# Sixteen sequences through six attention layers on one core: projections and feed-forward layers as pairs of 64-row matmuls, all eight PSUM banks as one ring

## The chip, the cores and the metric

One NeuronCore of a Trainium2 chip runs the whole program. The metric is the device time of one execution in microseconds (us), median of several. A measurement of this kernel can tell a change of about 0.3% from none.

## The reference, cut to what matters

Sixteen sequences of 256 tokens with 256 features go through six attention layers with 16 heads of 16 features each. Some layers have a feed-forward part. Cut to one layer:

```python
Q, K, V = x @ Wq.T, c @ Wk.T, c @ Wv.T        # c: the context, or x in self-attention (layers 2 and 4)
scores = einsum("bhqd,bhkd->bhqk", Q, K)      # plus masks: general (0), causal (2), lengths (2, 3)
attn = softmax(scores / sqrt(16))
x = layernorm(x + einsum("bhqk,bhkd->bhqd", attn, V) @ Wo.T)   # no Wo in layers 2 and 3
x = layernorm(x + act(x @ W1.T + b1) @ W2.T + b2)              # layers 1 and 5: 1024 wide, layer 3: 256 wide
```

## The kernel before, in words

A unit is one sequence in one attention layer: `n` runs from 0 to 95, `attention(n)` is `n // 16`. A unit is cut into steps, named by kind, unit and index:

- `xtr`, `xff`, `ctr`, `otr`, `ott`, `pvt`: transposes on TensorE of x, of the layernormed x, of the context, of the attention output (two steps, `otr` 0 and 1), of the scaled output, and of V in layer 0. Four 128x128 matmuls against `ident` each.
- `pq`, `pk`, `pvv`, `opr`: the projections Q, K, V and output.
- `nat` 0 to 7: scores of a pair of heads with queries on the partitions, from which VectorE takes the row maximum (`mx`, line 1307; in layer 0 partly a masked form, line 1301). `st` 0 to 7: the same scores transposed, which ScalarE exponentiates into `pt` (line 1037). Both are matmuls over 64 rows: one head of the pair lies on partitions 0 to 63, the other on 64 to 127, and each head's result goes to a PSUM bank of its own.
- `pvg` 0 and 1: attention times V, in four groups of 32 columns of the array (line 854). `pvout`: ScalarE copies the result to `ote`.
- `e0`: a small product that finds sequence lengths in layers 2 and 3.
- `ff1` 0 to 3, `ff2a` 0 to 2 and `ff2`: the feed-forward layers. In layers 1 and 5 they and in layers 2 and 4 the projections are computed from operands split in a rounded part and a rest, as three matmuls at the rounded precision instead of one in plain float32. In the profile both kinds are called f32. A matmul in plain float32 becomes two MATMUL instructions (two passes), a rounded one becomes one.

So the array is used in three shapes, shown in the profile ahead of the operand sizes: `128*128` (full array: transposes, projections, feed-forward), `64*128` (`nat`, `st`) and `128*32` (`pvg`, `e0`).

The order of the work on every engine is a table, `STEPS`: for each layer each step has a place in units (8 to a unit), and optionally other places for single engines. `plan()` adds `8 * n` and `Order` sorts. A step with a place `"q"` is issued on TensorE in two parts: part 0 at its own place and part 1 at the `"q"` place, so other steps may lie between them. In the kernel before the two parts are the two halves of the output (tokens or features 0 to 127 and 128 to 255), each of 256 columns in the same bank.

PSUM has eight banks of 512 float32 columns. Before, `ps_nat` has two, `ps_st` two, `ps_pv` one, and three are a ring `ps_misc` for all the rest. The next `nat` waits until VectorE has read the last one (`max_done`), the next `st` until ScalarE has read the last one (`exp_done`).

```python
for j in halves:                      # pq, pk in layers 1, 3 and 5, before
    for dk in range(2):
        last = nc.tensor.matmul(bank[:, j * S:(j + 1) * S], wv[:, dk, j * P:(j + 1) * P],
                                src[:, dk, :], start=dk == 0, stop=dk == 1)
```

Of the kernel before, what the change touches and what calls it, by code (L numbers as in the profile page):

```python
# [7 lines left out]
P = 128  # L8
B, S, D, H = 16, 256, 256, 16
HD = D // H  # L10
DF = 4 * D
NA = 6
# [18 lines left out]
MISC = 3  # L31
# [41 lines left out]
def w_pieces(a):  # L73
# [4 lines left out]
    0: [("ldt", 0, -23.0722), ("pq", 0, -10.5145, {"a": -11.9187}), ("pql", 0, -10.1072), ("pk", 0, -8.6981, {"a":  # L78
        -8.6385}), ("pkl", 0, -7.9888), ("kin", 0, -8.2233), ("qin", 1, -5.2344), ("qin", 0, -8.2358), ("kin", 1, -5.7617),
        ("pen", 0, -9.8123), ("pvv", 0, 0.7475, {"d": 0.4579}), ("pvt", 0, 4.2243, {"a": 3.4888}), ("pvt", 1, 7.2243, {"a":  # L80
        4.8512}), ("otr", 0, 17.3689, {"d": 17.0245}), ("pb", 0, 18.5644), ("otr", 1, 17.3875, {"d": 17.0609}), ("ott", 0,
        17.5054), ("opr", 0, 18.8675, {"d": 20.7955}), ("lnA", 0, 21.0455, {"g": 22.5079}), ("lnB", 0, 27.3239, {"g":
        30.4865}), ("nmt", 0, 4.81, {"g": 3.166}), ("pvout", 0, 12.4872), ("pvg", 0, 9.6187, {"q": 9.7016}), ("nmt", 1,
# [8 lines left out]
        ("qin", 1, -7.1117), ("qin", 0, -11.3952), ("kin", 1, -3.887), ("pvv", 0, 0.7691, {"q": 0.7862, "d": 0.6665}),  # L92
# [6 lines left out]
        41.0084, {"g": 45.0372}), ("msk", 0, 48.3061), ("nmt", 0, 4.7887, {"g": 3.2704}), ("pvout", 0, 11.3402), ("pvg", 0,  # L99
# [6 lines left out]
        ("hlo", 0, 28.5643), ("hlo", 1, 28.7505), ("hlo", 2, 31.6121), ("hlo", 3, 32.4921)],  # L106
    2: [("xtr", 0, -15.0784, {"a": -16.1489}), ("xtl", 0, -14.8701), ("pq", 0, -14.096, {"q": -14.0381, "a": -14.8795}),
# [64 lines left out]
def attention(n):  # L172

    return n // B


USERS = {"tld": "s", "wsp": "d", "wld": "s", "ldx": "s", "ldt": "s", "ldn": "s", "pen": "s", "nat": "pd", "st": "pa",
         "nmt": "dg", "pvout": "a", "pvg": "p", "pq": "pad", "pk": "pad", "pql": "d", "pkl": "d", "kin": "s", "qin": "s",
# [42 lines left out]
class Order:  # L221

    def __init__(self, stages):
# [13 lines left out]
        for e, part, *_ in sorted(self.by["p"] + self.by["q"] + freeing, key=lambda s: s[2:]):  # L237
            kind, n, i = e
            if kind in RELEASE:
                del held[RELEASE[kind], n, 0]  # L240
# [1343 lines left out]
```

## Time and profile before

| what | value |
|---|---|
| time, median of 3 runs | 2486.88 us (2486.25 to 2492.78) |
| the profiled execution's own time | 2489.72 us |
| its span, first to last instruction | 2487.9 us |
| mean granted TensorE clock | 0.991 |
| TensorE (PE) busy | 2393.9 us, 96% |
| VectorE (DVE) busy | 1926.6 us, 77% |
| ScalarE (ACT) busy | 1454.0 us, 58% |
| GpSimd (POOL) busy | 1104.9 us, 44% |

A row of the profile names the line of the kernel, the engine, the instruction, output <- inputs, the shape, and how many (x). PE is the matmuls, PEld the weight loads that run beside them. Matmuls overlap in the array: one of 0.28 us can start 0.12 us after the last. So what a group of matmuls costs is read from the end of the group before it (start + duration) to its own end, and is called its step here.

### The profile page before, as it was taken

How to read it: one execution, taken by the hardware profiler on the slowest of the kernel's cores; microseconds unless marked ns; L12 is line 12 of the kernel's file. 1: busy time of each engine (PE TensorE's matmuls, PEld its weight loads, DVE VectorE, ACT ScalarE, POOL GpSimd, SP SyncE). 2: the span in 40 equal slices, each digit the busy share in tenths (PEclk: the TensorE clock that was granted, in tenths of full speed). 3: DMA queues.
4: the chain of work that ended last, by engine and by line, in shares of the span. 5: the costliest groups of instructions: out<-in, count | busy, mean ns of one | idle time of the engine just before them, and what ended most of it. 6: DMA issues, size and time to landing. Idle time of an engine off the chain costs nothing.

```text
span 2487.9 us, 63230 instructions
## 1 busy us (share of the span) xinstructions
PE 2393.9 (96%) x24352; PEld 1855.5 (75%) x24352; DVE 1926.6 (77%) x4308; ACT 1454.0 (58%) x2321; POOL 1104.9 (44%) x1606
## 2 busy tenths in 40 slices
PE   5999999999999989999999999999999999999997
PEld 4766767688888868878776666667777778888886
DVE  6888988877778877777788888878789876666662
ACT  1444444565555544455556677677677777666664
POOL 1333434444444433455445677786445443222220
PEclk8999999999999999999999999999999999999998
DMA  5453343222111111232222322222422221111120
GB/s 168 107 157 89 98 102 81 94 75 67 63 63 63 63 43 48 76 106 87 89 92 94 98 92 83 72 82 91 136 93 99 99 76 63 63 63 63 59 84 13
DMA packets 138379, 208.55 MB, mean 84 GB/s; under 512 B 43857, under 2 KB 52321, under 8 KB 138082
## 3 DMA queue, kind: packets, MB, share of 16 engines
q1 hardware_dynamic: 113506, 201.03, 24.7%
q0 software_dynamic: 24576, 3.49, 1.1%
q8 instruction: 196, 3.21, 0.6%
q14 instruction: 101, 0.83, 0.1%
HBM read 40.70 MB, written 4.19 MB: 18 GB/s over the span
## 4 chain that ended last, share of the span: by engine, by line
PE 68%; DVE 9%; issue 2%; ACT 1%; POOL 1%; DMA 0%; DVEq 0%; ACTq 0%
PE ps_pv L854 9%; PE ps_st L677 8%; PE ps_nat L659 7%; PE ps_misc L770 5%; PE ps_misc L886 3%; DVE mx L1307 3%; PE ps_misc L809 3%; PE ps_misc L919 3%; PE ps_misc L954 2%; PE ps_misc L903 2%; PE ps_misc L865 2%; PE ps_misc L955 2%; PE ps_misc L956 2%; PE ps_misc L921 2%; PE ps_misc L920 2%
## 5 line engine op out<-in xcount | busy, mean ns | idle before, releaser
L1037 ACT ACTIVATE pt<-ps_st 128x1024 f32<-128x1024 f32 (+1 forms) x768 | 760.3, 990 | 656.2 <-PE ps_st L677 367.4
L1428 POOL DMA_DIRECT2D q_st<-shifts_t x768 | 456.4, 599 | 1062.7 <-DVE shifts_t L1319 1062.2
L1307 DVE TENSOR_REDUCE mx<-ps_nat 128x4 f32<-128x1024 f32 x560 | 679.8, 1214 | 185.0 <-PE ps_nat L659 166.6
L659 PE MATMUL ps_nat<-k_st,q_st 64*128 64x256 f32 (+1 forms) x3072 | 353.8, 308 | 36.2 <-DVE mx L1307 20.1
L677 PE MATMUL ps_st<-q_st,k_st 64*128 64x256 f32 (+1 forms) x3072 | 366.5, 317 | 10.0 <-ACT pt L1037 6.2
L854 PE MATMUL ps_pv<-pt,vaug 128*32 128x256 f32 (+1 forms) x6144 | 374.5, 376 | 0.0
L677 PEld LDWEIGHTS ps_st<-q_st,k_st 64*128 64x128 f32 x3072 | 231.5, 185 | 145.2 <-issue 106.3
L659 PEld LDWEIGHTS ps_nat<-k_st,q_st 64*128 64x128 f32 x3072 | 233.4, 186 | 111.3 <-issue 63.9
L854 PEld LDWEIGHTS ps_pv<-pt,vaug 128*32 128x32 f32 x6144 | 171.8, 110 | 124.2 <-ACT pt L1037 7.1
L1086 ACT ACTIVATE hT<-ps_misc,cols 128x256 f32<-128x256 f32 x288 | 121.3, 477 | 130.3 <-PE ps_misc L921 72.4
L919 PE MATMUL ps_misc<-xF_hi,up_hi 128*128 128x256 f32 x512 | 158.1, 309 | 14.1 <-DVE qk L1185 10.9
L1475 POOL TENSOR_TENSOR xn<-xn,tiles 128x512 f32<-128x512 f32 x128 | 165.9, 1296 | 10.0
L1474 POOL TENSOR_TENSOR xn<-xn,tiles 128x512 f32<-128x512 f32 x128 | 168.4, 1316 | 4.0 <-ACT xn L1048 2.6
L954 PE MATMUL ps_misc<-down_hi,hT_r 128*128 128x256 f32 x512 | 157.5, 308 | 7.1 <-DVE hT_r L1224 7.1
L1224 DVE TENSOR_TENSOR hT_r<-hT,hT_r 128x512 fp32r<-128x512 f32 x128 | 91.7, 727 | 72.4 <-ACT hT_r L1086 72.4
L1301 DVE CUSTOM_DVE_ANT_0 ps_nat<-ps_nat,on 128x256 f32<-128x256 f32 x320 | 125.5, 455 | 26.8 <-PE ps_nat L659 26.7
L920 PE MATMUL ps_misc<-xF_hi,weights_lo 128*128 128x256 f32 x512 | 145.8, 285 | 0.0
L921 PE MATMUL ps_misc<-xF_lo,up_hi 128*128 128x256 f32 x512 | 145.6, 284 | 0.0
L955 PE MATMUL ps_misc<-weights_lo,hT_r 128*128 128x256 f32 x512 | 145.2, 284 | 0.0
L956 PE MATMUL ps_misc<-down_hi,hT_r 128*128 128x256 f32 x512 | 144.5, 282 | 0.0
L1043 ACT ACTIVATE ote<-ps_pv 128x512 f32<-128x512 f32 x192 | 114.9, 598 | 41.6 <-PE ps_pv L854 41.6
L1413 POOL TENSOR_SCALAR rstd<-mv 128x2 f32<-128x2 f32 x144 | 32.2, 224 | 224.1 <-DVE mv L1113 219.5
(159 smaller groups left out, 5061.5 us busy)
## 6 DMA issues: line engine op xcount, KB each, us to landing
q_st<-qk SPq DMA_DIRECT2D x576, 128.0 KB
k_st<-qk SPq DMA_DIRECT2D x576, 128.0 KB, 2.1
q_st<-shifts_t POOLq DMA_DIRECT2D x768, 4.0 KB, 1.8
weights<-in_weights SPq DMA_DIRECT2D x19, 512.0 KB, 4.0
cT<-in_ctx_t SPq DMA_DIRECT2D x32, 256.0 KB, 2.8
cn<-in_ctx SPq DMA_DIRECT2D x32, 256.0 KB, 2.7
xT<-in_x_t SPq DMA_DIRECT2D x16, 256.0 KB, 3.2
xn<-in_x SPq DMA_DIRECT2D x16, 256.0 KB, 3.0
```

The source lines that it names most:

```text
L659: return nc.tensor.matmul(ps_nat[:, j, hf, 0:keys], lhs, rhs, start=hf == 0, stop=last)
L677: return nc.tensor.matmul(ps_st[:, j, kh, 0:S - q0], lhs, rhs, start=kh == first, stop=last)
L854: last = nc.tensor.matmul(ps_pv[32 * j:32 * j + 32, c, q0:S], vaug[:, rot, kh, slot, :], pt[:, at_p, side, kh * S:(kh + 1) * S - q0], star ...
L919: nc.tensor.matmul(out, up_hi[dk][:, cut], xF_hi[:, dk, :], start=dk == 0, stop=False)
L920: nc.tensor.matmul(out, lo[:, dk, cut], xF_hi[:, dk, :], start=False, stop=False)
L921: last = nc.tensor.matmul(out, up_hi[dk][:, cut], xF_lo[:, dk, :], start=False, stop=dk == 1)
L954: nc.tensor.matmul(out, h_hi, down_hi[:, ch, :], start=step == 0 and c == 0, stop=False)
L955: nc.tensor.matmul(out, h_hi, lo[:, ch, :], start=False, stop=False)
L956: last = nc.tensor.matmul(out, h_lo, down_hi[:, ch, :], start=False, stop=step == 3 and c == 3)
L1037: nc.scalar.activation(pt[:, g % PT_SLOTS, :, 0:used], ps_st[:].rearrange("p j a b -> p j (a b)")[:, :, 0:used], ACT.Exp, scale=SCALE).the ...
L1307: last = nc.vector.reduce_max(out, ps_nat[:], AX)
L1428: nc.gpsimd.dma_start(rows[:, b], shifts_t[32 * b:32 * b + 32, i, :]).then_inc(split_in[rot][i], 16)
```

## The change

Three things change together.

1. **Pairs of 64 rows.** `WIDE` lists the steps that now use the shape 64*128: beside `nat` and `st` all of `pq`, `pk`, `pvv`, `opr`, `ff1`, `ff2a` and `ff2`. A matmul over 128 rows becomes two over 64 rows, one on partitions 0 to 63, one on 64 to 127. In part 0 (`swap` 0) the upper rows add to output half 0 in the first bank and the lower rows to half 1 in the second bank. In part 1 it is the other way round. Since both row groups write to both banks in turn, part 1 waits on a semaphore (`rows_done`) that the last matmul of part 0 raises; in the long chain `ff2a` 0, 1, 2, `ff2` the steps 1 and 3 wait in this way for steps 0 and 2. Transposes, `pvg` and `e0` keep their shapes.
2. **One ring of eight banks.** `ps` holds all banks. `nat`, `st` and every wide step take two neighbouring banks, the rest one, always those that have been free longest by the order of the table. A step waits for the readers of the steps that last had its banks.
3. **A new table.** All places in `STEPS` change. By the sorting rule of `Order`, the steps of 96 units in the order of TensorE are 3472 (parts counted apart) before and 3536 after, since `pq`, `pk`, `pvv` and `opr` of layer 0 are now in two parts.

On VectorE, the scaling of `otr` in layers 0, 1, 4 and 5 reads the bank in two halves: two reciprocals for one, and outside layer 0 two multiplications for one. Other readers get the same elements from two banks instead of one.

```diff
-MISC = 3
+BANKS = 8
+WIDE = {"nat": range(NA), "st": range(NA), "pq": (0, 1, 2, 3, 4, 5), "pk": (0, 1, 2, 3, 4, 5), "pvv": (0, 1, 2, 3, 4, 5), "opr": (0, 1, 4, 5),
+        "ff1": (1, 3, 5), "ff2": (1, 3, 5), "ff2a": (1, 5)}
...
-        ("nat", 0, 0.1635, {"d": 0.599}), ("st",
-        0, 7.5268, {"a": 7.0873}), ("nat", 1, 1.7018, {"d": 1.7987}), ("st", 1, 8.1236, {"a": 7.4481}), ("nat", 2, 2.5189,
...
+        ("otr", 0, 15.9717, {"d": 16.9916}), ("otr", 1, 17.9472, {"d": 18.3718}), ("ott", 0, 18.7715, {"a": 19.3055}),
+        ("opr", 0, 20.5152, {"q": 20.7535, "d": 20.8617}), ("lnA", 0, 34.6135, {"g": 30.255}), ("lnB", 0, 57.1659, {"g":
...
+                taken = {b for banks in held.values() for b in banks}
+                age = {b: k for k, b in enumerate(turn) if b not in taken}
+                if wide(e):
+                    first = min((b for b in age if b + 1 in age), key=lambda b: (max(age[b], age[b + 1]), b))
+                    banks = [first, first + 1]
+                else:
+                    banks = [min(age, key=age.get)]
+                turn = [b for b in turn if b not in banks] + banks
+                self.before[e] = sorted({last[b] for b in banks if last[b]})
...
-        ps_nat = ctx.enter_context(nc.psum_tensor("ps_nat", [P, 2, 2, S], F32))
-        ps_st = ctx.enter_context(nc.psum_tensor("ps_st", [P, 2, 2, S], F32))
-        ps_pv = ctx.enter_context(nc.psum_tensor("ps_pv", [P, 2, S], F32))
-        ps_misc = ctx.enter_context(nc.psum_tensor("ps_misc", [P, MISC, 512], F32))
+        ps = ctx.enter_context(nc.psum_tensor("ps", [P, BANKS, 512], F32))
...
+                def open_bank(e, part=None):
...
+                    if part == 1 and wide(e):
+                        pe.wait_ge(rows_done, phases[e])
+                    if part != 1:
+                        for old in win.before[e]:
+                            if old[0] == "nat":
+                                pe.wait_ge(max_done, nth(old))
+                            elif old[0] == "st":
+                                pe.wait_ge(exp_done, nth(old))
+                            else:
+                                wait_out(pe, old)
+                    return ps[:, win.bank[e][0], :]
...
+                def both_rows(e, swap, lhs, rhs, start, stop):
+
+                    out = halves_of(e)
+                    if not wide(e):
+                        return nc.tensor.matmul(out[:, swap, :], lhs[swap], rhs[swap], start=start, stop=stop)
+                    for g in range(2):
+                        half, rows = g ^ swap, slice(GROUP * g, GROUP * g + GROUP)
+                        last = nc.tensor.matmul(out[:, half, :], lhs[half][rows], rhs[half][rows], start=start and not swap,
+                                                stop=stop and bool(swap))
+                    return last
...
-                            for j in halves:
-                                for dk in range(2):
-                                    last = nc.tensor.matmul(bank[:, j * S:(j + 1) * S], wv[:, dk, j * P:(j + 1) * P],
-                                                            src[:, dk, :], start=dk == 0, stop=dk == 1)
+                            for dk in range(2):
+                                last = both_rows(e, part, [wv[:, dk, j * P:(j + 1) * P] for j in range(2)], [src[:, dk, :]] * 2,
+                                                 dk == 0, dk == 1)
...
-                            th, quarter = step % 2, step // 2
+                            swap, quarter = (0, 1, 1, 0)[step], step // 2
...
+                            else:
+                                pe.wait_ge(rows_done, phases["ff2a", n, step - 1])
...
-                        link(nc.vector.reciprocal(rec[:, i], bank[:, :, :, HD]))
-                        if a in (2, 3):
+                        if not scaled_out(e):
+                            bank = bank.rearrange("p (f q) g (s w) -> p f q g s w", f=2, w=32)
+                            own = rec[:, i].rearrange("p f (q g s) -> p f q g s", q=2, g=2)
+                            for hf in range(2):
+                                last = nc.vector.reciprocal(own[:, hf], bank[:, hf, :, :, :, HD])
+                            link(last)
+                        else:
...
-                            dst = on[:].rearrange("p f (s d) -> p f s d", d=HD)
-                            last = nc.vector.tensor_tensor(dst[:, :, 8 * i:8 * i + 8, :], src, by, ALU.mult)
```

## Rows read from the trace of the kernel before

**Rows 1.** The page: busy time by engine, and the chain that ended last
```profile
PE 2393.9 (96%) x24352; PEld 1855.5 (75%) x24352; DVE 1926.6 (77%) x4308; ACT 1454.0 (58%) x2321; POOL 1104.9 (44%) x1606
PE 68%; DVE 9%; issue 2%; ACT 1%; POOL 1%; DMA 0%; DVEq 0%; ACTq 0%
```
**Rows 2.** The waits of PE alone: who for, us, times, longest
```profile
PE ps_nat L659 <- DVE mx L1307: 20.1, 28, 2.0
PE ps_misc L919 <- DVE qk L1185: 10.9, 4, 4.1
PE ps_nat L659 <- DMA k_st<-qk: 9.4, 13, 1.7
PE ps_misc L753 <- DMA weights<-in_weights: 8.9, 1, 8.9
PE ps_misc L954 <- DVE hT_r L1224: 7.1, 4, 2.8
PE ps_st L677 <- ACT pt L1037: 6.2, 9, 1.1
```
**Rows 3.** Timeline of PE: start us, duration us, line, matmuls (L954-956 feed-forward, rounded)
```profile
706.01 0.28 PE L955 MATMUL ps_misc<-weights_lo,hT_r 128*128 128x256 f32 x1
706.13 0.28 PE L956 MATMUL ps_misc<-down_hi,hT_r 128*128 128x256 f32 x1
706.34 0.50 PE L659 MATMUL ps_nat<-k_st,q_st 64*128 64x256 f32 x4
706.68 0.39 PE L677 MATMUL ps_st<-q_st,k_st 64*128 64x256 f32 x4
707.00 1.13 PE L770 MATMUL ps_misc<-cT,weights 128*128 128x256 f32 x4
...
709.27 0.28 PE L956 MATMUL ps_misc<-down_hi,hT_r 128*128 128x256 f32 x1
709.38 1.02 PE L770 MATMUL ps_misc<-cT,weights 128*128 128x256 f32 x4
```
**Rows 4.** Timeline of PE at 1403 and at 1412 us: transposes, attention times V
```profile
1402.83 0.59 PE L945 MATMUL ps_misc<-weights,hT 128*128 128x256 f32 x2
1403.26 0.60 PE L831 MATMUL ps_misc<-ident,cn 128*128 128x128 f32 x4
...
1405.00 0.40 PE L659 MATMUL ps_nat<-k_st,q_st 64*128 64x256 f32 x4
1405.33 1.07 PE L854 MATMUL ps_pv<-pt,vaug 128*32 128x256 f32 x16
...
1412.15 0.40 PE L659 MATMUL ps_nat<-k_st,q_st 64*128 64x256 f32 x4
1412.48 0.66 PE L865 MATMUL ps_misc<-ident,ote 128*128 128x128 f32 x4
```
**Rows 5.** Timeline of PE at 714 us and at 881 us: two more shapes
```profile
713.95 0.60 PE L865 MATMUL ps_misc<-ident,ote 128*128 128x128 f32 x4
714.48 1.93 PE L854 MATMUL ps_pv<-pt,vaug 128*32 128x256 f32 x32
...
881.14 0.40 PE L659 MATMUL ps_nat<-k_st,q_st 64*128 64x256 f32 x4
881.47 1.06 PE L780 MATMUL ps_misc<-qk,q0blk 128*32 128x256 f32 x8
```
**Rows 6.** Timeline at 1413 us: VectorE ends, the waiting `nat` starts (in brackets: idle before)
```profile
1413.72 1.22 DVE L1307 TENSOR_REDUCE mx<-ps_nat 128x4 f32<-128x1024 f32 x1
1414.99 0.50 PE L659 MATMUL ps_nat<-k_st,q_st 64*128 64x256 f32 x4 [1.00 <-DVE mx L1307]
```
**Rows 7.** VectorE groups: count, busy us, mean ns, idle before
```profile
L1323 DVE RECIPROCAL rec<-ps_misc 128x16 f32<-128x16 f32 x192 | 47.7, 249 | 49.3 <-PE ps_misc L865 47.7
L1343 DVE TENSOR_TENSOR on<-ps_misc,rec 128x256 f32<-128x256 f32 x96 | 40.8, 425 | 3.4
L1334 DVE TENSOR_TENSOR hbuf<-ps_misc,rec 128x128 f32<-128x128 f32 x64 | 15.6, 286 | 1.1
```
**Rows 8.** Busy us in the layers 0, 3 and 4: length, PE, PEld, DVE, ACT, POOL, clock
```profile
0.00:433.00 433.00, 397.94 (x4162) 284.01 (x4162) 359.51 (x1167) 179.72 (x226) 140.88 (x199) 0.98 0.44 115
...
1290.00:1652.00 362.00, 346.18 (x3146) 243.61 (x3146) 307.86 (x631) 248.29 (x384) 259.72 (x390) 1.00 0.26 87
1652.00:1957.00 305.00, 301.11 (x3036) 228.79 (x3037) 257.37 (x472) 213.15 (x299) 166.51 (x265) 0.99 0.30 101
```

More of the change, by code:

```diff
@@ L174, in attention, with wide @@
     return n // B
+TURNS = ("xtr", "xff", "ctr", "otr", "ott", "pvt")
+def wide(e):
+    return attention(e[1]) in WIDE.get(e[0], ())
 USERS = {"tld": "s", "wsp": "d", "wld": "s", "ldx": "s", "ldt": "s", "ldn": "s", "pen": "s", "nat": "pd", "st": "pa",
@@ L212, in plan @@
     return out
-MISC_KINDS = ("pq", "pk", "pvv", "pvt", "ctr", "e0", "otr", "ott", "opr", "xtr", "xff", "ff1", "ff2a", "ff2")
-RELEASE = {"len": "e0", "pql": "pq", "pkl": "pk", "xtl": "xtr", "xfl": "xff"}
+IN_BANKS = ("nat", "st", "pvg", "pq", "pk", "pvv", "pvt", "ctr", "e0", "otr", "ott", "opr", "xtr", "xff", "ff1", "ff2a", "ff2")
+RELEASE = {"pvout": "pvg", "len": "e0", "pql": "pq", "pkl": "pk", "xtl": "xtr", "xfl": "xff"}
 class Order:
@@ L230, in __init__ @@
         halved = {e for e, *_ in self.by["q"]}
-        self.kinds, self.bank = {}, {}
+        self.kinds, self.bank, self.banks, self.before, self.ready = {}, {}, {}, {}, {}
         for e in self.order:
             self.kinds.setdefault(e[0], []).append(e)
-        uses, held = [0] * MISC, {}
-        turn = list(range(MISC))
-        freeing = [s for s in self.by["d"] if s[0][0] in RELEASE and not (s[0][0] == "xfl" and attention(s[0][1]) == 5)]
+        uses, fills, held, last = [0] * BANKS, [0] * BANKS, {}, [None] * BANKS
+        turn = list(range(BANKS))
+        freeing = [s for s in self.by["a"] + self.by["d"]
+                   if s[0][0] in RELEASE and not (s[0][0] == "xfl" and attention(s[0][1]) == 5)]
         for e, part, *_ in sorted(self.by["p"] + self.by["q"] + freeing, key=lambda s: s[2:]):
@@ L617, in filled, with half_done @@
+                def half_done(e, last):
+                    phases[e] = len(phases) + 1
+                    last.then_inc(rows_done, 1)
                 def filled(e, last, part=None):
-                    if part != 0:
-                        last.then_inc(misc_ready[win.bank[e][0]], 1)
+                    if part == 0 and wide(e):
+                        half_done(e, last)
+                    elif part != 0:
+                        last.then_inc(bank_full[win.bank[e][0]], 1)
                 def need_cT(n):
@@ L806, in _ @@
                         wv = w("v" + str(a), D)
-                        for hf in halves:
-                            for dk in range(2):
-                                last = nc.tensor.matmul(bank[:, hf * D:(hf + 1) * D], src[:, dk, hf * P:(hf + 1) * P],
-                                                        wv[:, dk, :], start=dk == 0, stop=dk == 1)
+                        for dk in range(2):
+                            last = both_rows(e, part, [src[:, dk, hf * P:(hf + 1) * P] for hf in range(2)], [wv[:, dk, :]] * 2,
+                                             dk == 0, dk == 1)
                         filled(e, last, part)
@@ L882, in _ @@
                         wo = w("o" + str(a), D)
-                        for th in halves:
-                            for c in range(2):
-                                lhs = (ot0 if a == 0 else ot)[:, c, th * P:(th + 1) * P]
-                                last = nc.tensor.matmul(bank[:, th * D:(th + 1) * D], lhs, wo[:, c, :], start=c == 0, stop=c == 1)
+                        for c in range(2):
+                            lhs = [(ot0 if a == 0 else ot)[:, c, th * P:(th + 1) * P] for th in range(2)]
+                            last = both_rows(e, part, lhs, [wo[:, c, :]] * 2, c == 0, c == 1)
                         filled(e, last, part)
@@ L924, in _ @@
                         wu = w("u" + str(a), D)
[L925 to L929 removed]
+                        for dk in range(2):
+                            last = both_rows(e, part, [wu[:, dk, (2 * i + c) * P:(2 * i + c + 1) * P] for c in range(2)],
+                                             [xF[:, dk, :]] * 2, dk == 0, dk == 1)
                         filled(e, last, part)
@@ L940, in _ @@
                                 pe.wait_ge(d3_made, 1)
-                            for th in halves:
-                                out = bank[:, th * D:(th + 1) * D]
-                                nc.tensor.matmul(out, ones_b[:], d3_b[:], start=True, stop=False)
-                                for ch in range(2):
-                                    last = nc.tensor.matmul(out, hT[:, ch, th * P:(th + 1) * P], wd[:, ch, :], start=False, stop=ch == 1)
+                            both_rows(e, part, [ones_b[:]] * 2, [d3_b[:]] * 2, True, False)
@@ L957, in _ @@
-                            if kind == "ff2a" and i == 1:
+                                ch = 4 * quarter + c
+                                for at, down in ((4, down_hi), (4, lo), (0, down_hi)):
+                                    for g in range(2):
+                                        th, rows = g ^ swap, slice(GROUP * g, GROUP * g + GROUP)
+                                        last = nc.tensor.matmul(out[:, th, :], hT_r[rows, c + at, th * P:(th + 1) * P], down[rows, ch, :],
+                                                                start=step == 0 and c == 0 and at == 4 and down is down_hi,
+                                                                stop=step == 3 and c == 3 and at == 0)
@@ L958, in _ @@
+                            if step == 1:
                                 last.then_inc(quarter_done, 1)
+                            elif kind == "ff2a":
+                                half_done(e, last)
                         if kind == "ff2":
```

314 lines of the change are left out of this document (163 added, 151 removed), and 113 rows, old and new, of the table STEPS.

## The prediction, made before the changed kernel ran

> **What bounds the kernel now.** I read the page first: PE is busy for 96% of the span and holds 68% of the chain that ended last, no other engine more than 9% [rows 1]. PE's own idle time is 94 us (2487.9 - 2393.9), and its list of waits has nothing large: 20.1 us for the row maxima, 10.9 us for banks that VectorE released late, the rest start-up and small things [rows 2]. So PE's own stream sets the time. What that stream consists of is read from its timeline by steps, end of one group to end of the next.
>
> Rounded matmuls on the full array start 0.12 us apart (706.01, 706.13). `nat` after them ends at 706.84, 0.43 us after 706.41, though it is only two pairs; `st` behind it, in the same shape, ends 0.23 us later. A pair of 64-row matmuls thus takes 0.117 us, the same as one full matmul over the same data, and coming from the full array cost 0.20 us. The Q/K projection in plain float32 behind `st` ends 1.06 us after it, while the same four matmuls behind a full-array step take 0.85 us (710.40 - 709.55): 0.20 us again [rows 3]. Transposes take 0.44 us behind a full-array step and 0.59 us behind `nat`: 0.15 us. `pvg` takes 1.00 us behind `nat` [rows 4], and two of them, 32 matmuls, 1.86 us, so 0.86 us each and 0.14 us for the change [rows 5].
>
> So every change of shape costs PE 0.14 to 0.20 us in which it does nothing useful, and which the page counts as busy, because the last matmuls are still running out. Sorting the old table by the rule of `Order` gives 1647 changes of shape: 770 into 64 rows, 274 into 32 columns, 197 into transposes, 406 into projections and feed-forward on the full array. At the prices above that is some 302 us. All steps at their price within a shape, and these, make about 2354 us; the other 134 us of the span are 13 us before the first matmuls end, 3 us after the last, and 118 us of waits and of the half clock that follows them.
>
> The Trainium skill (TensorEngine Tiling, Key Properties) says that changing the tiling mode drains the engine. The trace agrees and gives the price, 0.14 to 0.20 us.
>
> **The change part by part.**
>
> Fewer changes of shape. The new table, sorted by the same rule, has 1016: 454 into 64 rows, 260 into 32 columns, 302 into transposes, none into full-array projections. That saves 316 x 0.20 + 406 x 0.20 + 14 x 0.14 - 105 x 0.15 = 130.6 us. Every one lies on PE, the engine that sets the end.
>
> The pairs themselves. The 6624 MATMUL instructions of the widened steps become 13248. For rounded operands a pair costs 0.117 us against 0.118, nothing [rows 3]. For plain float32 no 64-row pair is in the trace. Nearest are two plain matmuls in different column groups: `e0`, eight instructions, ends 0.99 us after `nat` (882.53 - 881.54), which is 0.14 us for the change and 0.85 us for four slots of 0.21 us; two at a time, then, at the rate of one [rows 5]. `pvg` runs four at a time at that rate. From below nothing can be gained, since the columns to stream are the same; from above, without overlap, each of 2304 plain instructions would cost 0.215 us more. I take nothing, as the nearest row has it.
>
> The Trainium skill (TensorEngine Tiling, Instruction Overhead) speaks against this: about 60 cycles of overhead for each matmul. By its figure 6624 more would cost 6624 x 60 / 2.4 GHz = 166 us, an estimate. The `nat` and `st` rows show no such cost.
>
> Waiting for itself. Part 1 must not start before part 0 has left the array, and PE gets this from a semaphore of its own. There are 576 such waits (512 second parts, and two in each of 32 `ff2a` chains). No engine of the trace waits for itself in this way on PE, so the price comes from a wait for another: VectorE ends at 1414.94, and the `nat` that waited ends at 1415.49, 0.55 us later, instead of the 0.235 us that its two pairs take in a running stream: 0.315 us [rows 6]. Behind the waiting instruction stands all of PE's queue, since it is in order, with the loads of weights too. From below: at least what a change of shape costs, 0.20 us. I take 0.318 (0.315 for rounded, a little more for plain). Where other steps lie between the parts they cover it. In the new table 319 second parts (or chain steps) follow directly on their first part: `ff1` 115, `pvv` 63, `pq` 52, `pk` 51, `opr` 33, five of the rest. That is 319 x 0.318 = 101.4 us. In 81 more, one `nat` or `st` of 0.235 us lies between and 0.083 us stay open: 6.7 us. The other 176 cost nothing. Sum 108.2 us, and this pays back most of what fewer changes of shape bring. At 0.20 us it would be 64 us.
>
> Together PE gets 22 us shorter. It is not even: by layers 0 to 5 about -2, -5, -18, -7, +3 and +8 us, as layer 5 has many `ff1` and layer 4 short steps.
>
> The ring. `nat` and `st` no longer wait for their one buffer. A wait of 1.00 us as at 1414.99 recurs at one `nat` in each of the 16 units of layer 3 [rows 6], some 16 of the 20.1 us [rows 2]; there the new order gives other banks. But wide steps hold two banks for one, and by the new order the distance from the last user of a bank to the next is in many places about 1.4 us, just above a maximum of 1.22 us [rows 6], as before. Part of what is gained comes back elsewhere. From 118 us of waits I leave 107.
>
> VectorE. Of 192 `otr`, 128 now need a second reciprocal: 128 x 0.249 = 31.9 us. 96 multiplications become two of half the size: 96 x (2 x 0.286 - 0.425) = 14.1 us [rows 7]. So VectorE gets 46 us more, 1973 us or 80% of the new span. The cover is its own idle time; in layers 3 and 4 it is busy for 85% and 84% already (307.86 of 362, 257.37 of 305) [rows 8]. What is late next is `ott` in layer 4, which comes about 1 us after `otr` 1 in the new table, while scaling takes about 1.2 us. I put 6 us on the path for it. The readers on ScalarE get the same number of elements: nothing. GpSimd and the queues for DMA issue the same work at other places, with GpSimd at 44% [rows 1]: nothing.
>
> **The sum**, against the profiled execution: 2489.7 - 130.6 + 108.2 - 11 + 6 = 2462.3 us. The median of the runs shown is 2.8 us below that execution, so 2459.5, say **2460 us**, 1.1% faster.
>
> **The rivals.**
>
> *The order by VectorE (slower).* The same place, VectorE's in-order queue, decides otherwise: it is the second engine, its work grows by 46 us, and PE's idle time next to it was tuned away by placing each `nat` just late enough. If all 46 us and not 6 reach PE, in layers 0, 3, 4 and 5, the time is 2500 us. The change is slower than before from 27 us beyond my term on. For it: 83 to 85% busy in three layers [rows 8]. Against it: PE's three longest waits for VectorE come to 38.1 us now [rows 2], and the self-waits give VectorE time.
>
> *The wait for itself is as cheap as a change of shape.* Then the term is 64 and not 108 us: 2416 us. For it: both let the array run dry. Against it: a semaphore must be raised and seen, and after a change of shape the next load starts before the last matmul has ended.
>
> *The ring takes most waits away.* If of 118 us only 60 stay, with my price for the self-wait: 2460 - 47 = 2413 us. For it: more banks between writer and reader. Against it: most of these waits are at the start, at deliveries by DMA, and at transitions between layers, where a bank is not what is missing [rows 2].
>
> *Pairs don't run side by side in plain float32*, so that the rewriting doesn't do what it says: 2304 x 0.215 = 495 us more, 2955 us; a fixed cost of each added matmul would be in between. If each of the 6624 cost 0.025 us, the time were 2626 us. The Trainium skill's section on instruction overhead, named above, gives about this one. Against both: the rows of `nat`, `st` and `e0` [rows 3, 5].
>
> **How the numbers follow.** My sum 0.50, with a range of its own from 2435 to 2485. VectorE 0.20. Cheap self-wait 0.13. Ring 0.12. Pairs that don't overlap or a cost for each 0.05. The range must take in the cheaper cases, down to 2408, and most of VectorE's, up to 2500; outside are the 0.05 and some of both ends. A measurement of this kernel tells about 0.3%, 7.5 us. Faster by more than that (below 2479): 0.13 and 0.12, most of the 0.50 (0.42), and little of VectorE's (0.03): 0.70. Within: 0.12. Slower: 0.18.
>
> **What would show it.** In the new profile: 30976 MATMUL instructions, the projections all in shape 64*128; a second part directly behind its first ends about 0.32 us later than in a running stream, 400 times; a pair in plain float32 starts 0.215 us after the last. PE shows more idle time than 94 us, as a self-wait may be counted as such. VectorE about 1973 us busy. The prediction is wrong if the self-wait costs 0.20 or 0.4 us, if PE's waits for VectorE grow above 90 us, or if the distance of plain pairs is above 0.22 us.

## The result, and the profile after

The changed kernel takes 2500.03 us (median of 7 runs, 2491.09 to 2502.12), the kernel before, beside it, 2486.88 us (7 runs). The ratio, taken over all runs, is 1.004, 95% interval 1.0023 to 1.0057: 0.4% slower (0.5% by the two medians alone). The forecast was 2460 us, 1.1% faster. The profiled execution took 2500.03 us with a span of 2498.2 us at a clock of 0.992.

The page of the changed kernel: busy time, and the chain that ended last by engine and by line (it answers to [rows 1]).
```profile
PE 2378.1 (95%) x30976; PEld 1894.0 (76%) x30976; DVE 1900.8 (76%) x4532; ACT 1464.1 (59%) x2321; POOL 1104.7 (44%) x1606
PE 83%; DVE 7%; issue 4%; ACT 2%; DMA 2%; SPq 1%; POOL 1%; DVEq 0%; ACTq 0%
```
PE is still what sets the time, more than before (83% of the chain, 68% before). It is busy 16 us less, but its idle time has gone from 94 to 120 us (2498.2 - 2378.1), as the prediction had it. The 30976 matmuls are the number forecast. VectorE has not grown: 1900.8 us, and not 1973.

PE's waits in the changed kernel: who for, us, times, longest (they answer to [rows 2]).
```profile
PE ps L687 <- PE ps L687: 18.7, 118, 0.2
PE ps L687 <- DMA weights<-in_weights: 9.3, 1, 9.3
PE ps L1026 <- DVE hT_r L1299: 5.4, 3, 2.4
PE ps L738 <- DVE mx L1383: 5.2, 6, 2.0
```
PE's largest wait is now for itself. The wait of `nat` for the row maxima has fallen from 20.1 us in 28 places to 5.2 in 6. The 18.7 us are only the part of the self-wait in which no matmul shows; the rest hides in "busy", as the timeline makes plain.

Timeline of PE in the changed kernel at 706 us, `ff1` in rounded numbers, part 1 directly behind part 0:
```profile
705.28 0.50 PE L756 MATMUL ps<-q_st,k_st 64*128 64x256 f32 x4
705.62 0.28 PE L687 MATMUL ps<-xF_hi,up_hi 64*128 64x256 f32 x2
705.73 0.28 PE L687 MATMUL ps<-xF_hi,weights_lo 64*128 64x256 f32 x2
...
706.21 0.28 PE L687 MATMUL ps<-xF_lo,up_hi 64*128 64x256 f32 x2
706.55 0.39 PE L687 MATMUL ps<-xF_hi,up_hi 64*128 64x256 f32 x2
706.77 0.29 PE L687 MATMUL ps<-xF_hi,weights_lo 64*128 64x256 f32 x2
...
709.20 0.50 PE L756 MATMUL ps<-q_st,k_st 64*128 64x256 f32 x4 [0.41 <-ACT hT_r L1161]
709.54 1.03 PE L687 MATMUL ps<-weights,cT 64*128 64x256 f32 x8
```
`ff1` follows `st` without a gap, pairs 0.12 us apart, where the full array had cost 0.20 us at each such place [rows 3]. The plain projection ends 0.87 us after `st` (710.57 - 709.70): four pairs at 0.217 us, side by side as assumed. But between 706.21 and 706.55 lie 0.34 us instead of 0.12, and the pair after is 0.22 us behind. Together that is some 0.33 us lost to the self-wait.

Transposes, `pvg` and `nat` in the changed kernel (they answer to [rows 4, 5]):
```profile
1412.74 0.43 PE L756 MATMUL ps<-q_st,k_st 64*128 64x256 f32 x4
1413.10 0.66 PE L674 MATMUL ps<-ident,cn 128*128 128x128 f32 x4
1413.68 1.93 PE L927 MATMUL ps<-pt,vaug 128*32 128x256 f32 x32
1415.55 0.51 PE L738 MATMUL ps<-k_st,q_st 64*128 64x256 f32 x4
```
Ends at 1413.17, 1413.76, 1415.61 and 1416.06: 0.59 us for the transposes, 1.85 for 32 matmuls of `pvg`, 0.45 for `nat`. These are the prices of before, within 0.02 us.

Groups of VectorE in the changed kernel: count, busy us, mean ns, idle before (they answer to [rows 7]).
```profile
L1419 DVE TENSOR_TENSOR on<-ps,rec 128x128 f32<-128x128 f32 x192 | 46.9, 286 | 3.3
L1403 DVE RECIPROCAL rec<-ps 128x8 f32<-128x8 f32 x256 | 34.9, 178 | 55.8 <-PE ps L674 55.6
L1407 DVE RECIPROCAL rec<-ps 128x16 f32<-128x16 f32 x64 | 15.9, 248 | 2.4 <-PE ps L674 1.4
L1193 DVE TENSOR_SCALAR xn<-xn,mv,rstd 128x256 f32<-128x256 f32 x96 | 35.1, 409 | 0.6
L1329 DVE TENSOR_TENSOR q0col<-qk 128x2 f32<-128x2 f32 x32 | 4.9, 153 | 0.1
```
A reciprocal of half the size costs 178 ns and not 249. By mean durations the split adds 13.6 us there (256 x 0.178 + 64 x 0.248 - 192 x 0.249) and not 31.9, and 14.1 at the multiplications; by busy time, since neighbours overlap, only 3.1 and 6.1 us. The last two rows give back 51 us against the same groups in the kernel before (the last section has why):
```profile
L1118 DVE TENSOR_SCALAR xn<-xn,mv,rstd 128x256 f32<-128x256 f32 x96 | 63.4, 701 | 2.5 <-POOL rstd L1414 1.9
L1254 DVE TENSOR_TENSOR q0col<-qk 128x2 f32<-128x2 f32 x32 | 28.1, 879 | 0.6
```

To see where the time is, every step of PE is priced as in the prediction: end of step minus end of the step before, minus the step's price within its shape, minus the price of a change of shape where there is one. The steps at their own price make 2054.2 us in every kernel of this study. What is left over is sorted by place: at second parts (and second chain steps) directly behind their first; at those with one step between; everywhere else, which is waits for other engines and the half clock behind them (1.2 GHz granted instead of 2.4 for some 45 us before and 39 us after, two thirds of it in the first 47 us, where PE idles until the first transfers land, and in the last 32 us). The 13 to 15 us at both ends are not in it. The table is of the profiled executions; the profiled one of later_fixed_banks is 3.7 us above its median, those of one_wait and no_self_wait are 2.7 and 4.5 us below theirs.

| kernel | median us | changes of shape (us) | directly behind: count, us | one between, us | elsewhere, us |
|---|---|---|---|---|---|
| before | 2486.9 | 1647 (299.8) | none | none | 119.5 |
| the forecast for after | 2460 | 1016 (171.4) | 319, 101.4 | 6.7 | 113 |
| after | 2500.0 | 1016 (171.1) | 319, 138.5 | 14.3 | 106.2 |
| one_wait | 2473.8 | 1016 (171.1) | 319, 110.3 | 7.8 | 112.2 |
| no_self_wait | 2388.4 | 1016 (171.1) | 319, 5.4 | 3.0 | 134.7 |
| one_reciprocal | 2493.3 | 1016 (171.1) | 319, 136.0 | 14.3 | 102.2 |
| both_small | 2471.5 | 1016 (171.1) | 319, 108.6 | 9.0 | 112.8 |
| full_array | 2551.7 | 2097 (388.2) | none | none | 93.7 |
| apart | 2491.0 | 1016 (171.1) | 38, 15.6 | 20.2 | 215.3 |
| later_scores | 2582.8 | 1016 (171.1) | 46, 18.6 | 27.5 | 295.9 |
| later_fixed_banks | 2475.5 | 1016 (171.1) | 46, 17.6 | 32.5 | 188.4 |
| earlier_fixed_banks | 2496.0 | 1016 (171.1) | 85, 30.4 | 16.7 | 207.8 |

The rows of before and after say at once which term is off: the self-wait, 152.8 us and not 108.2. The rest of this text is about why, and about what it would bring to be rid of it.

### The profile page after: what moved, and what is told of

Read it like the earlier page. It is cut to its first block, busy times and chain, and to the rows that moved or that the text cites. A ratio compares the mean times of both kernels' runs of the same rounds, so it can differ in the third digit from the quotient of the medians.

```text
span 2498.2 us, 77552 instructions
## 1 busy us (share of the span) xinstructions
PE 2378.1 (95%) x30976; PEld 1894.0 (76%) x30976; DVE 1900.8 (76%) x4532; ACT 1464.1 (59%) x2321; POOL 1104.7 (44%) x1606
## 4 chain that ended last, share of the span: by engine, by line
PE 83%; DVE 7%; issue 4%; ACT 2%; DMA 2%; SPq 1%; POOL 1%; DVEq 0%; ACTq 0%
PE ps L687 34%; PE ps L927 12%; PE ps L756 9%; PE ps L738 8%; PE ps L674 8%; PE ps L1026 8%; PE ps L746 2%; PE ps L761 2%; DVE mx L1383 1%; DMA q_st<-shifts_t 1%; PE ps L856 1%; DVE qk L1246 1%; DVE stats L1185 1%; ACT hT_r L1161 1%; POOL q_st L1510 0%
## 5 line engine op out<-in xcount | busy, mean ns | idle before, releaser
L1111 ACT ACTIVATE pt<-ps 128x1024 f32<-128x1024 f32 (+1 forms) x768 | 748.5, 989 | 328.0 <-PE ps L746 162.5
L1383 DVE TENSOR_REDUCE mx<-ps 128x4 f32<-128x1024 f32 x560 | 677.3, 1218 | 171.5 <-PE ps L738 167.8
L756 PE MATMUL ps<-q_st,k_st 64*128 64x256 f32 (+1 forms) x3072 | 373.2, 322 | 23.1 <-DMA q_st<-shifts_t 5.3
L927 PE MATMUL ps<-pt,vaug 128*32 128x256 f32 (+1 forms) x6144 | 373.5, 374 | 2.0 <-DVE qk L1258 1.2
L738 PE MATMUL ps<-k_st,q_st 64*128 64x256 f32 (+1 forms) x3072 | 361.2, 313 | 10.3 <-DVE mx L1383 5.2
L756 PEld LDWEIGHTS ps<-q_st,k_st 64*128 64x128 f32 x3072 | 249.1, 186 | 111.9 <-issue 73.8
L738 PEld LDWEIGHTS ps<-k_st,q_st 64*128 64x128 f32 x3072 | 254.2, 187 | 56.2 <-issue 38.9
L927 PEld LDWEIGHTS ps<-pt,vaug 128*32 128x32 f32 x6144 | 177.6, 109 | 123.7 <-issue 15.5
L1026 PE MATMUL ps<-down_hi,hT_r 64*128 64x256 f32 x2048 | 214.6, 288 | 5.7 <-DVE hT_r L1299 5.4
L1026 PEld LDWEIGHTS ps<-down_hi,hT_r 64*128 64x128 f32 x2048 | 175.3, 188 | 10.7 <-DVE hT_r L1299 8.3
```

Of the source, the lines that this page charges most:

```text
L738: return nc.tensor.matmul(scores_of(e)[:, j, hf, 0:keys], lhs, rhs, start=hf == 0, stop=last)
L756: return nc.tensor.matmul(scores_of(e)[:, j, kh, 0:S - q0], lhs, rhs, start=kh == first, stop=last)
L927: last = nc.tensor.matmul(bank[32 * j:32 * j + 32, c * S + q0:(c + 1) * S], vaug[:, rot, kh, slot, :], pt[:, at_p, side, kh * S:(kh + 1) * ...
L1026: last = nc.tensor.matmul(out[:, th, :], hT_r[rows, c + at, th * P:(th + 1) * P], down[rows, ch, :], start=step == 0 and c == 0 and at == ...
L1111: nc.scalar.activation(pt[:, g % PT_SLOTS, :, 0:used], scores_of(e).rearrange("p j a b -> p j (a b)")[:, :, 0:used], ACT.Exp, scale=SCALE) ...
L1383: last = nc.vector.reduce_max(out, found, AX)
```

## Experiments

### What a self-wait costs

**one_wait.** In the changed kernel part 1 of a projection, of `opr`, of `ff1` 0 and of `ff2` in layer 3 waits for `rows_done`, and once more for its source, which part 0 has already waited for. Here part 1 waits for `rows_done` alone.
```diff
-                        if a == 0:
-                            pe.wait_ge(ot0_ready, ...)
+                        if part == 1:
+                            pass
+                        elif a == 0:
+                            pe.wait_ge(ot0_ready, ...)
```


> The changed kernel, but a second part repeats none of the waits that its first part has already passed (for transposes, for the context, for weights); it waits only for rows_done. Theory A (a second wait on the same instruction costs about 0.065 us even when it is long fulfilled): 199 projections and 32 ff1 directly behind their first part start their loads about 0.057 us instead of 0.12 to 0.13 us after its end, some 15 us less than the changed kernel, about 2485 us. Theory B (fulfilled waits are free, the difference between ff1 and the projections comes from plain float32): 2500 us as the changed kernel.

Measured: 2473.84 us, ratio 0.9944 (0.9932 to 0.9957). That is 26 us below the changed kernel and 0.6% faster than before. The theory of a costly second wait holds, that of free fulfilled waits is out; the 15 us expected were too few, since they reckoned with the delay of the load alone. The same second part, `pk` of a unit of layer 4, in three kernels that differ in its waits (the third, further down, also in the bank that each half of the rows adds to). First the changed kernel, matmuls and then weight loads:
```profile
1761.09 0.31 PE L687 MATMUL ps<-xT_hi,weights_lo 64*128 64x256 f32 x2
1761.56 0.39 PE L687 MATMUL ps<-xT_hi,qkv_hi 64*128 64x256 f32 x2
...
1761.53 0.21 PEld L687 LDWEIGHTS ps<-xT_hi,qkv_hi 64*128 64x128 f32 x2 [0.32 <-issue]
```
One_wait:
```profile
1741.11 0.28 PE L687 MATMUL ps<-xT_hi,weights_lo 64*128 64x256 f32 x2
1741.45 0.39 PE L687 MATMUL ps<-xT_hi,qkv_hi 64*128 64x256 f32 x2
...
1741.45 0.19 PEld L687 LDWEIGHTS ps<-xT_hi,qkv_hi 64*128 64x128 f32 x2 [0.27 <-PE ps L687]
```
The last matmul of part 0 ends at 1761.41 and at 1741.39, as the profile models its end. With one wait the next load starts 0.06 us after that end, with two 0.12 us after it, though the second wait was long fulfilled. By all places of this kind, the median of the load's start is 0.056 to 0.070 us after the end with one wait and 0.118 to 0.132 with two. The loss against a running stream is 0.33 to 0.34 us with one wait; with two it is 0.42 us for rounded and 0.50 us for plain operands. In the changed kernel only `ff1` 1 to 3 and the chain steps had one.

**before_self_wait.** The old kernel, on the full array, with the same kind of wait between the two parts of its halved steps and nothing else changed.
```diff
+                    if part == 1:
+                        pe.wait_ge(rows_done, phases[e])
...
-                    if part != 0:
+                    if part == 0:
+                        phases[e] = len(phases) + 1
+                        last.then_inc(rows_done, 1)
+                    else:
```


> The kernel before with one thing added: the second part of pq, pk, pvv, opr, ff1 and ff2 waits on TensorE for the end of its first part; full-array matmuls, old table, old banks. 266 second parts follow directly on their first part. Theory A (the wait for itself costs what the changed kernel shows, 0.33 us where it is the only wait and 0.42 us where another, long fulfilled wait stands beside it): about 98 x 0.33 + 168 x 0.42 = 103 us more, about 2590 us. Theory B (the price is that of a change of shape, 0.20 us, and the rest of the changed kernel's time is in something else): 53 us more, 2540 us. Theory C (the time lies with VectorE, and pauses of TensorE are absorbed by waits that it has anyway): under 30 us more.

Measured: 2567.40 us, ratio 1.0322 (1.0308 to 1.0336), 80.5 us more. At the 266 second parts directly behind their first stand 97.1 us, 0.365 each (0.33 with one wait, 0.39 with two); some 17 us are missing again at other waits. So the price of a single wait, 0.33 us, has nothing to do with pairs or the ring, and the 0.20 us of a change of shape is excluded. With two waits the full array loses less (0.39) than the pairs (0.42 and 0.50).

**no_self_wait.** one_wait without any of the 576 self-waits. So that nothing has to wait, a row group adds to the same bank in both parts; every output half then is a sum over the wrong operands.
```diff
-                        last = nc.tensor.matmul(out[:, half, :], lhs[half][rows], rhs[half][rows], ...
+                        last = nc.tensor.matmul(out[:, g, :], lhs[half][rows], rhs[half][rows], ...
```


> one_wait with all 576 self-waits gone, in its order and with its banks. So that nothing has to wait, each row group adds to the same bank in both parts (the lower rows always to the first bank, the upper rows always to the second), so that every output half gets the sum over the wrong operands; matmuls, shapes, loads and readers are the same in number and size. In one_wait the self-waits cost 118 us by their places (110.3 behind their own first part, 7.8 with one step between). If TensorE's stream alone sets the time, all of it comes back: 2473.8 - 118 = 2356 us. Rival (the other engines are hardly behind TensorE, and what a self-wait gives back is waited for elsewhere, as in later_fixed_banks, where 68 us less at second parts brought 0 us): over 2450 us. In between, the share that comes back is read off: half of it is 2415.

Measured: 2388.37 us, ratio 0.9609 (0.9592 to 0.9627), 85.5 us below one_wait. The same `pk`:
```profile
1685.00 0.31 PE L685 MATMUL ps<-xT_hi,weights_lo 64*128 64x256 f32 x2
1685.11 0.32 PE L685 MATMUL ps<-xT_hi,qkv_hi 64*128 64x256 f32 x2
```
Nothing is lost between 1685.00 and 1685.11. By the table 109.7 us (118.1 - 8.4) go at the second parts and 22.5 us come back elsewhere: some four fifths of what a self-wait costs reach the end, one fifth had only taken the place of waits for other engines. Neither pure theory held: not 2356, not above 2450.

### VectorE

**one_reciprocal.** The scaling of `otr` as in the kernel before: one reciprocal over the bank, one multiplication outside layer 0.
```diff
-                            for hf in range(2):
-                                last = nc.vector.reciprocal(own[:, hf], bank[:, hf, :, :, :, HD])
-                            link(last)
+                        link(nc.vector.reciprocal(rec[:, i], bank[:, :, :, HD]))
```


> The changed kernel with the scaling of otr on VectorE as before: one reciprocal of 16 elements for two of 8, and one multiplication for two outside layer 0, some 23 us less VectorE work by the two profiles. Theory A (VectorE's added work is off the path): 2495 to 2500 us. Theory C (VectorE sets the end): 20 us or more better than the changed kernel, below 2480 us.

Measured: 2493.26 us, ratio 1.0027 (1.0018 to 1.0036), 7 us below the changed kernel by the medians, near the 6 us of my term. By the ratios it is 3 us, and the two intervals overlap, so the size of this effect isn't shown. The rival in which VectorE carries the whole loss, 20 us or more, is out.

### Pairs

**full_array.** The changed kernel, its order, its ring and its second parts, with only `nat` and `st` in 64 rows; no self-waits are needed then.
```diff
-WIDE = {"nat": range(NA), "st": range(NA), "pq": (0, 1, 2, 3, 4, 5), ...
+WIDE = {"nat": range(NA), "st": range(NA)}
```


> The changed kernel's table and ring of eight banks, but projections and feed-forward as full-array matmuls, in one bank each and without the wait for themselves. In this order that gives 2097 changes of shape. Theory A (shape changes at 0.14 to 0.20 us and self-waits explain the two kernels): steps 2054 us, changes 388 us, waits for others some 110 us as in the changed kernel, 15 us at both ends: about 2568 us, so the pairs are worth some 70 us in this order. Theory D (the pairs themselves cost, by issue or by not overlapping): less than 2500 us, as the full-array form is then the better one.

Measured: 2551.69 us, ratio 1.0262 (1.0248 to 1.0276). In this order pairs with their self-waits save 52 us, and by the table that is 217.1 us fewer changes of shape, against 152.8 of self-waits and 12.5 of other waits: 51.8. The prices of shape changes were right and add up. The expected 2568 us were 16 too many, since 93.7 us of other waits are left and not 110. The ring with the old table, the other half of this separation, wasn't tried, so no run separates the ring from the new order.

### Covering the self-wait with other steps

If the price can't fall, another step can stand between the parts. Six kernels exchange neighbours in PE's order; all have one_wait's edit too.

**apart.** A `nat`, `st` or the start of another group that follows a second part is put in front of it; if there is none, a `nat` or `st` that stands before the first part is put behind that.
```diff
+            if x and shape(x[0]) == 64 and (x[0][0] in ("nat", "st") or ...):
+                seq[k + 1], seq[k + 2] = seq[k + 2], seq[k + 1]
+            elif y and y[0][0] in ("nat", "st") and k > 1:
+                seq[k - 1], seq[k] = seq[k], seq[k - 1]
```


> As one_wait, and the order on TensorE changed so that a second part hardly ever follows directly on its first part: it changes places with the nat, st or first part behind it, or the nat or st ahead of the first part changes places with the first part. 35 of 316 adjacent pairs remain, 1016 changes of shape as before. Theory A (the self-wait is what ate the gain: 153 us of the changed kernel's steps in all): 35 x 0.33 us and some 0.1 us for each of the 281 others remain, about 40 us, so 110 us less than the changed kernel, 2390 us, up to 2430 if banks held longer make new waits. Theory C (VectorE is the bound): less than 30 us better than the changed kernel, above 2470 us.

Measured: 2490.95 us, ratio 1.0012 (1.0003 to 1.0021), 17 us slower than one_wait, and 101 us above the 2390 of the theory. The self-waits fell from 118 to 36 us, and 103 us of other waits came. At the 205 `nat` and `st` that are issued one place earlier 67 us of it stand, at the `nat` and `st` that stayed 17, at those issued later nothing, the rest at other steps. PE's waits in this kernel:
```profile
PE ps L784 <- DVE qk L1274: 10.0, 8, 1.8
PE ps L766 <- ACT hT_r L1197: 9.9, 13, 0.8
PE ps L766 <- DVE mx L1419: 9.2, 18, 2.0
```
A score step (L766 and L784 here) that comes earlier finds its two banks not yet read.

**later_scores** moves score steps only to later places: one in front of a first part goes behind it. **later_one_reciprocal** has one_reciprocal's edit as well.
```diff
-            if x and shape(x[0]) == 64 and (x[0][0] in ("nat", "st") or ...):
-                seq[k + 1], seq[k + 2] = seq[k + 2], seq[k + 1]
-            elif y and y[0][0] in ("nat", "st") and k > 1:
+            if y and y[0][0] in ("nat", "st") and k > 1:
                 seq[k - 1], seq[k] = seq[k], seq[k - 1]
```


> As apart, but no nat or st is ever issued earlier: where a nat or st stands ahead of an adjacent pair of parts, it goes between them, and otherwise only a first part may change places with a second one. 43 adjacent second parts of 316 are left. In apart the 205 nat and st that had moved ahead of a second part waited 67 us more, for banks not yet read. Theory A (self-wait and those bank waits are the two terms): 43 x 0.33 us and about 0.08 us for each of the others remain of 118 us, and no bank waits are added, so about 85 us less than one_wait (2474 us), 2390 us, up to 2430 with waits that a faster TensorE uncovers. Theory E (the readers on VectorE and ScalarE set the pace of the ring, and whatever TensorE saves turns into waiting for banks, as in apart): 2465 to 2490 us.

> later_scores with the scaling of otr on VectorE as in the kernel before, some 23 us less work there. In the changed kernel this was worth 7 us. Theory A: 5 to 10 us less than later_scores. Theory E (VectorE sets the pace once the self-waits are gone): 15 to 25 us less than later_scores.

Measured: 2582.78 us, ratio 1.0383 (1.0368 to 1.0397), and 2582.03 us, ratio 1.0380 (1.0366 to 1.0394). The theory fell badly, and so did VectorE as the pacemaker: 23 us less work there brought 0.75 us. Timeline of later_scores at 1827 us, PE and then VectorE:
```profile
1827.11 0.40 PE L784 MATMUL ps<-q_st,k_st 64*128 64x256 f32 x4
1829.29 1.07 PE L958 MATMUL ps<-pt,vaug 128*32 128x256 f32 x16 [1.77 <-DVE qk L1298]
...
1828.46 0.68 DVE L1298 TENSOR_TENSOR qk<-ps,qk 128x512 fp32r<-128x512 f32 x1
```
`pvg` waits 1.77 us for `pkl`, which has nothing to do with its data. The ring is dealt out in the sorted order; after the exchanges `pvg` of unit 70 stood at a bank whose last user was `pk` of unit 73, issued just before it and read late. In the changed kernel that predecessor is `st` 7 of unit 70, long read. Of 2736 steps that take banks 1268 had another predecessor than in one_wait, and at these stood 162 of the 182 us that had come at first parts and whole steps.

**later_fixed_banks.** The exchanges of later_scores, made after the banks are dealt out, so that each step keeps bank and predecessor; an exchange with one's own predecessor is left out.
```diff
+        self.by["p"] = set_apart(self.by["p"], self.before)
```


> Second parts apart as in later_scores (43 of 576 stand directly behind their own first part, 316 in one_wait), but every step keeps the bank and the predecessor in its bank that it has in the changed kernel; only the order in which TensorE issues is moved. Theory F (later_scores lost time because the moved order handed out other banks: of the 182 us of excess that it added to one_wait's, 162 us lay at steps whose predecessor in the bank had changed): those 162 us go, so about 2583 - 162 = 2421 us, between 2410 and 2440. Rival G (the order itself costs it: score steps one place later starve VectorE and ScalarE): 2550 to 2583 us as in later_scores. Half of each: 2500.

Measured: 2475.48 us, ratio 0.9954 (0.9941 to 0.9966). 107 us came back by holding the banks: in later_scores the dealing out was the cause. The same place in later_fixed_banks has no wait (the group of 28 matmuls is `pvg` 0.32 us after `st`):
```profile
1767.20 0.40 PE L780 MATMUL ps<-q_st,k_st 64*128 64x256 f32 x4
1767.53 1.72 PE L954 MATMUL ps<-pt,vaug 128*32 128x256 f32 x28
```
But my number was 2421, and against one_wait nothing is won at all. At the 269 second parts that got a cover 68.4 us are gone; at the 269 first parts now issued one place earlier 53.5 us have come (0.2 each on average, but 49 of them at 108 places and hardly any at half of the places), and at steps that stayed in their place 34; those moved later got 11 us shorter. PE's waits in this kernel:
```profile
PE ps L711 <- ACT pt L1143: 16.4, 51, 1.1
PE ps L711 <- DVE mx L1415: 9.4, 9, 4.1
```
The first of these, for the exponentials that have read the bank, is 1.5 us in 4 places in one_wait.

**earlier_fixed_banks.** The exchanges that move score steps and starts of groups forward, with banks kept.
```diff
-BACK, NEXT = True, False
+BACK, NEXT = False, True
```


> As apart, only with the bank handed out as in the changed kernel, and no step moved in front of its own predecessor: 82 second parts stay directly behind their first. In apart only 10 of the 104 us of added excess lay at steps whose predecessor had changed, so here the banks are not the reason: score steps issued one place earlier wait for ScalarE or VectorE to have read the bank. Theory: 2475 to 2488 us, at most some 15 us better than apart (2490.95). Rival (the bank handed out is the reason here too): under 2440 us.

Measured: 2496.00 us, ratio 1.0032 (1.0021 to 1.0043), above the 2475 to 2488 of the theory, though the rival (under 2440) is out too. At second parts moved later 67.9 us are gone; at the 133 `nat` moved forward 48.4 us have come, at the 72 `st` 18.5. Forward moves lose in either way of dealing banks.

**both_small** is one_wait with one_reciprocal's edit, **later_fixed_banks_all** is later_fixed_banks with it. Their edits are those shown above.

> one_wait (2473.84, -26 us) and one_reciprocal (2493.26, -7 us) together, the order and the banks of the changed kernel. If they add: 2467 us. If the VectorE work was hidden behind the same self-waits: 2473.

> later_fixed_banks with one reciprocal over both banks as well. If later_fixed_banks is at 2421 and TensorE still waits for ott and opr banks there: 2414; if VectorE has slack as in later_scores (2582.78 against 2582.03): the same as later_fixed_banks within 1 us.

Measured: 2471.46 us, ratio 0.9937 (0.9923 to 0.9951), and 2473.63 us, ratio 0.9945 (0.9932 to 0.9957). both_small is the fastest kernel that computes the reference, 0.6% below before, but its interval overlaps with that of one_wait: of the 7 us of one_reciprocal some 2 are left once the second wait is gone, which these runs can't tell from none.

## Why the prediction was wrong, point by point

**Changes of shape, -130.6 us: right.** 1016 of them at 171.1 us, with 299.8 before: -128.7. full_array closes with the same prices.

**Pairs cost nothing: right.** 0.12 us for a rounded pair, 0.217 for a plain one. The rival of 2955 or 2626 us is out. The steps at their own price make 2054.2 us with 24352 matmul instructions as with 30976. The Trainium skill's section on instruction overhead (TensorEngine Tiling), which the prediction weighed, is not borne out for these pairs: the estimate by its figure, 166 us more, is seen nowhere.

**The self-wait, "319 x 0.318 = 101.4 us" and 6.7 us: the step that failed, mis-sized by 44.6 us.** The mechanism, the places and their number were right, and for a single wait so was the price: 0.33 us measured, 109.7 us in all, in the difference of one_wait and no_self_wait by place. What I left out is that most second parts pass two waits. I had read the price off a `nat` that waits for one other engine, and took the second, long fulfilled wait to be free, without saying so. It delays the next load by another 0.06 us, and the step by 0.09 us (rounded) or 0.16 us (plain): 34.7 us by place (152.8 - 118.1), 26 us of the time. A further 8.4 us stand at these places even without any self-wait. All in all a second part directly behind its first lost 0.43 us (138.5 / 319) and not 0.318, which is beyond the 0.4 us that the prediction named as a sign of being wrong.

**The ring, 118 to 107 us, and VectorE's 6 us: right in sum, in part by luck.** 106.2 us elsewhere and not 113. The wait for the maxima did go (20.1 to 5.2 us). But VectorE did not get the 46 us on which the 6 us rest: its instructions beside GpSimd got shorter at their new places, a term that the prediction had put at nothing. What the ring, the new order and this relief each brought was not separated. The rival "the ring takes most waits away" (2413) is out, and so is the cheap self-wait (2416). The rival by VectorE (2500) has the right number for a wrong reason: VectorE is busy 26 us less, not 46 more, and its split work is worth 7 us.

The sum with the measured terms: 2462.3 + 44.6 - 6.8 = 2500.1, where the profiled execution took 2500.03. (It has to close nearly so, as the table puts every step somewhere.) With the second wait gone the kernel is at 2473.8, within my case's own range of 2435 to 2485, and faster than before. So the sign turned on a second wait that was already fulfilled.

**An assumption that the runs show to be too simple:** terms of the self-wait and of waits for others were added as if they were independent. Without self-waits 134.7 us are waited elsewhere, with them 112.2. That a fifth is given back made the error in the time smaller than in the term.

What stays open: in later_fixed_banks the first parts moved forward wait for ScalarE and VectorE to have read their banks, which the list of waits names for some 21 of the 53.5 us (25.8 in the two rows, 4.7 in one_wait's); the rest is spread too thin to be named. Whether a table made for one wait and for its prices would get at the 118 us that are left wasn't tried.

## What to carry to other kernels

Count the waits in front of each instruction, not only the one that is fulfilled last: where an engine has just been stopped, a second wait that was fulfilled long ago is not free, and a part that repeats the waits of the part before it can simply drop them. A step moved to cover one wait is exposed to the next one, so a cover is worth its price only if the moved step has slack of its own: look at when its bank was read. Where resources are dealt out in the order of the steps, an exchange of two neighbours redeals everything behind it; hold the assignment while testing an order.

## What the runs showed of the hardware

- TensorE that waits for a semaphore which its own last matmul raises starts its next load 0.06 us after that matmul's end and loses 0.33 to 0.34 us against a running stream, on the full array (before_self_wait) as with pairs (one_wait). A second, fulfilled wait brings the load to 0.12 us after it, in both shapes.
- In pairs, plain operands suffer more from the second wait (0.50 us lost) than rounded ones (0.42 us), at nearly the same delay of the load; on the full array both lose 0.39 us. No run here separates the reason.
- A VectorE instruction between SBUF tiles can be stretched by GpSimd. In the kernel before, two groups of the same instruction, the first beside GpSimd's additions (third row, running into the next one), the second with GpSimd idle:
```profile
708.80 2.66 DVE L1118 TENSOR_SCALAR xn<-xn,mv,rstd 128x256 f32<-128x256 f32 x2
723.40 0.73 DVE L1118 TENSOR_SCALAR xn<-xn,mv,rstd 128x256 f32<-128x256 f32 x2
...
708.66 1.29 POOL L1474 TENSOR_TENSOR xn<-xn,tiles 128x512 f32<-128x512 f32 x1
```
  1.3 us each and not 0.4. Of the 96 in the kernel before, 32 run beside these additions and take 1.37 us (median), the other 64 at most 0.42. The row maxima, which read PSUM, take 1.22 us beside them as elsewhere. In the changed kernel none of the 96 runs beside them, and none is above 0.42 us. That is where VectorE's forecast 46 us went: the new places of these steps avoid GpSimd's additions, which was read from the traces and not tested by a run of its own.
